# A graph-attention layer with a mixture of experts on one core: the edge stage by destination tile in 34 fixed chunks, with the node update, the router and the dispatch inside its loop

## The reference

```python
x = layernorm(x)                              # inner input; the residual adds the raw x
hh = (x @ W).reshape(n, 8, 32)
s = leaky_relu(s_src[src] + s_dst[dst])       # per head
alpha = softmax of s over the edges of one dst
out = scatter(hh[src] * alpha) + x
x = x_raw + elu(layernorm(out) * gamma + beta)
y = layernorm(x)
logits = y @ gate_w + gate_b                  # 16 experts, top 2, softmax over the two
moe = sum over the 2 chosen e: w_e * (relu(y @ w1[e] + b1[e]) @ w2[e] + b2[e])
x = x + layernorm(y + moe) * gamma2 + beta2
```

## Time and profile before

| what | us |
|---|---|
| median of 3 runs (3936.52 to 3939.79) | 3939.26 |
| span of the profiled execution, first to last instruction | 3974.2 |
| first to last gather of the edge stage begins | 159.9 to 2926.0 |
| stage4 and route together | 2935 to 3300 |
| clearing and lists, experts, last stage | 3300 to 3974 |

### The profile page before, as it was taken

The page is one execution under the profiler, slowest core; times in us unless marked ns, Lnnn a source line. Parts: engine busy times, 40 slices in busy tenths (PEclk is TensorE's granted clock), DMA queues, the critical chain, the costliest instruction groups (busy, mean ns, idle before and its releaser), DMA issues. The chain is left out here.

```text
span 3974.2 us, 63681 instructions
## 1 busy us (share of the span) xinstructions
PE 2665.6 (67%) x11030; PEld 2067.8 (52%) x11031; DVE 1943.5 (49%) x5747; ACT 1154.1 (29%) x4391; POOL 1958.4 (49%) x1920
## 2 busy tenths in 40 slices
PE   5377777777777777776777677777740444999900
PEld 4356556566556655555556555555530442666600
DVE  6355555555545554555545555555569322222246
ACT  4222222222222222222222222222244221333333
POOL 1255565655555665565656556656645451000065
PEclk8676776766777776677777767667765556999955
DMA  4333333333333333333333333333340323333333
GB/s 128 92 82 86 83 85 85 87 84 85 83 83 85 85 87 81 84 84 84 86 84 85 84 83 86 86 81 84 86 129 0 122 74 94 97 96 96 96 99 102
DMA packets 199124, 348.04 MB, mean 88 GB/s; under 512 B 56146, under 2 KB 134976, under 8 KB 199092
## 3 DMA queue, kind: packets, MB, share of 16 engines
q0 software_dynamic: 90432, 259.73, 23.8%
q1 hardware_dynamic: 99636, 87.69, 7.2%
q10 hardware_dynamic: 9024, 0.30, 0.1%
HBM read 301.28 MB, written 46.28 MB: 87 GB/s over the span
## 5 line engine op out<-in xcount | busy, mean ns | idle before, releaser
L849 POOL DMA_INDIRECT gat<-table,idx x1680 | 1663.8, 990 | 1130.7 <-ACT idx L886 638.4
L954 PE MATMUL ps_sum<-msg,hot 128*128 128x264 f32 x3348 | 1363.3, 546 | 0.0
L945 PE MATMUL ps_hot<-ident,hot 128*128 128x128 f32 x1680 | 463.7, 370 | 756.3 <-DVE hot L987 668.6
L954 PEld LDWEIGHTS ps_sum<-msg,hot 128*128 128x128 f32 x3348 | 809.5, 267 | 117.1
L945 PEld LDWEIGHTS ps_hot<-ident,hot 128*128 128x128 f32 x1680 | 266.8, 186 | 1073.3 <-DVE hot L987 676.6
L1002 DVE TENSOR_TENSOR acc<-acc,ps_sum 128x264 f32 x836 | 357.3, 427 | 787.7 <-PE ps_sum L954 446.9
L935 PEld LDWEIGHTS ps_look<-dst_tab,hotT 128*128 128x128 f32 x3356 | 644.7, 268 | 4.7 <-issue 1.3
L935 PE MATMUL ps_look<-dst_tab,hotT 128*128 x3356 | 605.8, 298 | 0.9 <-ACT hotT L905 0.9
L905 ACT ACTIVATE hotT<-ps_hot 128x256 f32<-128x256 f32 x840 | 322.6, 384 | 950.0 <-remote 401.2
L1005 DVE TENSOR_TENSOR msg<-gat,msg 128x512 f32<-128x512 f32 x838 | 577.3, 689 | 17.3 <-ACT msg L900 14.9
L900 ACT ACTIVATE msg<-score 128x16 f32<-128x16 f32 x838 | 180.9, 216 | 1088.7 <-DVE score L993 735.6
(11 more groups left out here) (270 smaller groups left out, 1687.0 us busy)
## 6 DMA issues: line engine op xcount, KB each, us to landing
gat<-table,idx POOLq DMA_INDIRECT x1680
w_sb<-in_L_ffn_w_dram SPq DMA_DIRECT2D x8, 2048.0 KB, 16.5
xt<-dispatched SPq DMA_DIRECT2D x111, 128.0 KB, 2.1
b_t<-in_L_ffn_b_dram SPq DMA_DIRECT2D x109, 128.0 KB, 3.0
expert_out<-o_sb SPq DMA_DIRECT2D x105, 128.0 KB, 1.7
table<-rows SPq DMA_DIRECT2D x49, 128.0 KB, 1.7
x_all<-in_x_dram SPq DMA_DIRECT2D x6, 896.0 KB, 10.3
out_dram<-normed SPq DMA_DIRECT2D x6, 896.0 KB, 4.3
```

What stands on the lines that cost most here:

```text
L849: pool.indirect_dma_start(gat[:, k, j, :], None, table, bass.IndirectOffsetOnAxis(ap=idx[:, k, j:j + 1], axis=0)).then_inc(landed[k], 16)
L945: last = pe.transpose(ps_hot[k % 2][:, j * P:(j + 1) * P], hot[:, k, j, :], ident[:, :])
L954: last = pe.matmul(ps_sum[(k - SUMS) % 2][:, 0:SUM], hot[:, (k - SUMS) % BODY, j, :], msg[:, (k - SUMS) % MSGS, j, :], start=(j == 0), sto ...
```

## The change

The schedule of steps is gone from the edge stage. Its loop now goes over the 49 destination tiles, and each tile takes a window of exactly 34 chunks of 128 edges from the place where its first edge stands in the sorted list (`lo_i`); an edge of another tile in the window gets no one-hot column. Partition p holds 34 edges that follow each other. The window is worked in four groups of 9, 9, 8 and 8 chunks, and one VectorE instruction serves a whole group.

Edges past the window go through `overflow`, which is simple and works one chunk after another, in passes of four. The counts give one such chunk here, so it runs one pass of four chunks. `stage1` finds the first edges with 39 small matmuls and more passes over the edge list, and writes padded copies of the edges to DRAM (`src_pad`, `dst_pad`, and `dst_half` in 16 bits).

The transposes of the one-hot matrices are gone: SyncE loads the window's destinations as one row into all 128 partitions (`dst_row`), and two ScalarE instructions over 4,352 elements turn it into the transposed one-hot matrix `hotT` in bf16. The lookup multiplies that with the destination scores split into three bf16 parts (48 columns), which VectorE adds up. In each of the large VectorE multiplies, compares and adds one operand lies in PSUM (`weight`, `iota`, `looked`). `ps_sum` adds up all 34 chunks of a tile, and the accumulator is added once a tile.

The work of `stage4` and `route` is cut into pieces of one tile (`class Finish`). In tile t of the loop stand pieces for tiles t-1, t-2 and t-3; `last_tiles` does what remains. Both weight loads stand there now, in four quarters each, and TensorE waits in `stage6` for the quarter that its expert needs.

```diff
+NEVER = 20000.0
+WCH = 34
+GROUPS = (9, 9, 8, 8)
+GSTART = (0, 9, 18, 26)
...
-    def step(k, g, head):
-        if not head:
-            pool.wait_ge(msg_ready, g - (BODY - 1))
-        pool.wait_ge(idx_ready, g + 1)
-        pool.sem_inc(pool_turn, 1)
-        for j in range(2):
-            pool.indirect_dma_start(gat[:, k, j, :], None, table,
-                                    bass.IndirectOffsetOnAxis(ap=idx[:, k, j:j + 1], axis=0)).then_inc(landed[k], 16)
...
-        dve.tensor_tensor(hot[:, k, :, :], node_iota[:, :].unsqueeze(1).to_broadcast([P, 2, P]),
-                          rel[:, k, :].unsqueeze(2).to_broadcast([P, 2, P]), ALU.is_equal).then_inc(hot_ready, 1)
...
-        dve.tensor_tensor(msg[:, m, :, 0:D].rearrange("p j (h d) -> p j h d", d=HD),
-                          gat[:, (k - WEIGH) % BODY, :, 0:D].rearrange("p j (h d) -> p j h d", d=HD),
-                          msg[:, m, :, D:SUM].unsqueeze(3).to_broadcast([P, 2, HEADS, HD]),
-                          ALU.mult).then_inc(msg_ready, 1)
...
+# in build(), between stage2 and stage3
+        with nc.cleanup_on_exit():
+            bounds(nc, table, schedule, src_pad, dst_pad, ident, node_iota, neg_first, dst_tab, dst_split,
+                   counts, seg_max)
+            overflow(nc, table, schedule, src_pad, dst_pad, acc, ident, node_iota, neg_first, dst_tab, counts)
+    stage3(nc, table, src_pad, dst_pad, dst_half, dispatched, finish, node_iota, node_id, neg_main, dst_split,
+           lo_i)
...
+# stage3, SyncE
+        lo = sp.value_load(lo_i[0:1, bass.ds(t, 1)], min_val=0, max_val=E)
+        if not head:
+            sp.wait_ge(hotT_ready, t)
+            sp.sem_inc(sp_turn, 1)
+        sp.dma_start(dst_row[:, :], dst_half[bass.ds(lo, WIN)].unsqueeze(0).to_broadcast([P, WIN])).then_inc(row_in, 16)
+        for g in range(NG):
+            if not head:
+                sp.wait_ge(landed[g], t * (16 * GROUPS[g]))
+                sp.sem_inc(sp_turn, 1)
+            sp.dma_start(idx[g][:, :], of_group(src_pad, lo, g)).then_inc(idx_in[g], 16)
+        if not head:
+            sp.wait_ge(rel_ready, t)
+            sp.sem_inc(sp_turn, 1)
+        sp.dma_start(dst_t[:, :], dst_pad[bass.ds(lo, WIN)].rearrange("(p e) -> p e", e=WCH)).then_inc(dst_in, 16)
+# stage3, GpSimd
+    def tile(t, head, old, last=False):
+        for g in range(NG):
+            pool.wait_ge(idx_in[g], t * 16 + 16)
+            pool.sem_inc(pool_turn, 1)
+            if not head:
+                pool.wait_ge(msg_ready, (t - 1) * NG + g + 1)
+                pool.sem_inc(pool_turn, 1)
+            for k in range(GROUPS[g]):
+                pool.indirect_dma_start(gat[:, GSTART[g] + k, :], None, table,
+                                        bass.IndirectOffsetOnAxis(ap=idx[g][:, k:k + 1], axis=0)).then_inc(landed[g], 16)
+            if g == 0 and old >= 3:
+                finish.send(pool, t - 3, dispatched, pool_turn)
+# stage3, ScalarE
+    def rows(t, head):
+        act.wait_ge(row_in, t * 16 + 16)
+        if not head:
+            act.wait_ge(look_done, t * NG)
+        act.activation(hotT[:, :], dst_row[:, :], ACT.Abs, bias=neg_id[:, bass.ds(t, 1)]).then_inc(apart_ready, 1)
+        act.wait_ge(apart_ready, t + 1)
+        act.activation(hotT[:, :], hotT[:, :], ACT.Relu, bias=1.0, scale=-1.0).then_inc(hotT_ready, 1)
+    def tile(t, head, old, last=False):
+        if old >= 1:
+            finish.norm_inner(act, t - 1)
+            finish.root_inner(act, t - 1)
+            if old >= 2:
+                finish.root_outer(act, t - 2)
+            act.preload_act_table(ACT.Exp)
+        for g in range(NG):
+            m, n = g % 2, GROUPS[g]
+            if g == 1 and old >= 1:
+                finish.centre(act, t - 1)
+            if g == 1 and old >= 2:
+                finish.norm_outer(act, t - 2)
+                finish.turned(act, t - 2, ps_t)
+            if g == 2 and old >= 1:
+                finish.lower(act, t - 1)
+            if g == 2 and old >= 2:
+                finish.odds(act, t - 2)
+            if g == NG - 1 and not last:
+                rows(t + 1, False)
+            act.wait_ge(score_ready, t * NG + g + 1)
+            if not (head and g < 2):
+                act.wait_ge(sum_done, t * NG + (g - 1))
+            act.activation(weight[:, m, 0:n, :], score[:, m, 0:n, :], ACT.Exp).then_inc(weight_ready, 1)
+            act.activation(msg[:, m, 0:n, D:SUM], score[:, m, 0:n, :], ACT.Exp).then_inc(denom_ready, 1)
+# stage3, TensorE
+    def look(t, g, head):
+        n, m = GROUPS[g], g % 2
+        if g == 0:
+            pe.wait_ge(hotT_ready, t + 1)
+        if not (head and g < 2):
+            pe.wait_ge(look_read, t * NG + (g - 1))
+        for k in range(n):
+            last = pe.matmul(ps_look[m][:, k * SPLIT * 2 * HEADS:(k + 1) * SPLIT * 2 * HEADS],
+                             by_chunk[:, GSTART[g] + k, :],
+                             dst_split[:, bass.ds(t, 1), :, :].rearrange("p t c h -> p (t c h)"),
+                             start=True, stop=True)
+        last.then_inc(look_done, 1)
+    def total(t, g, head):
+        n, m = GROUPS[g], g % 2
+        pe.wait_ge(hot_ready, t * NG + g + 1)
+        pe.wait_ge(msg_ready, t * NG + g + 1)
+        pe.wait_ge(denom_ready, t * NG + g + 1)
+        if g == 0 and not head:
+            pe.wait_ge(added, t)
+        for k in range(n):
+            last = pe.matmul(ps_sum[:, 0:SUM], hot[:, m, k, :], msg[:, m, k, :],
+                             start=(g == 0 and k == 0), stop=(g == NG - 1 and k == n - 1))
+        last.then_inc(sum_done, 1)
+    def tile(t, head, old, last=False):
+        for g in range(NG):
+            if g < NG - 1:
+                look(t, g + 1, head)
+            elif not last:
+                look(t + 1, 0, False)
+            if g == 1 and old >= 2:
+                finish.vote(pe, t - 2, ps_route)
+            total(t, g, head)
+            if g == 0 and old >= 2:
+                finish.turn(pe, t - 2, ps_t)
+            if g == 1 and old >= 2:
+                finish.ranks(pe, t - 2, ps_route)
+# stage3, VectorE
+    def columns(t, head):
+        dve.wait_ge(dst_in, t * 16 + 16)
+        if not head:
+            dve.wait_ge(hot_ready, t * NG)
+        dve.tensor_scalar(rel[:, :], dst_t[:, :], neg_main[:, bass.ds(t, 1)], None, ALU.add).then_inc(rel_ready, 1)
+    def group(t, g, head):
+        n, m, j = GROUPS[g], g % 2, GSTART[g]
+        early = head and g < 2
+        dve.wait_ge(look_done, t * NG + g + 1)
+        dve.tensor_reduce(looked[:, 0:n, :], ps_look[m][:, 0:n * SPLIT * 2 * HEADS].rearrange(
+            "p (j c h) -> p j h c", c=SPLIT, h=2 * HEADS), AX.X, ALU.add).then_inc(look_read, 1)
+        dve.wait_ge(landed[g], (t + 1) * (16 * n))
+        dve.wait_ge(look_read, t * NG + g + 1)
+        dve.tensor_tensor(both[:, 0:n, :], gat[:, j:j + n, D:ROW], looked[:, 0:n, :], ALU.add).then_inc(both_ready, 1)
+        dve.wait_ge(both_ready, t * NG + g + 1)
+        dve.tensor_reduce(score[:, m, 0:n, :], both[:, 0:n, :].rearrange("p j (c h) -> p j h c", h=HEADS),
+                          AX.X, ALU.max).then_inc(score_ready, 1)
+        if not early:
+            dve.wait_ge(sum_done, t * NG + (g - 1))
+        if g == 0:
+            dve.wait_ge(rel_ready, t + 1)
+        dve.tensor_tensor(hot[:, m, 0:n, :], iota.unsqueeze(1).to_broadcast([P, n, P]),
+                          rel[:, j:j + n].unsqueeze(2).to_broadcast([P, n, P]), ALU.is_equal).then_inc(hot_ready, 1)
+        dve.wait_ge(weight_ready, t * NG + g + 1)
+        dve.tensor_tensor(msg[:, m, 0:n, 0:D].rearrange("p j (h d) -> p j h d", d=HD),
+                          gat[:, j:j + n, 0:D].rearrange("p j (h d) -> p j h d", d=HD),
+                          weight[:, m, 0:n, :].unsqueeze(3).to_broadcast([P, n, HEADS, HD]),
+                          ALU.mult).then_inc(msg_ready, 1)
+    def tile(t, head, old, last=False):
+        columns(t, head)
+        if old >= 1:
+            finish.sums(dve, link, t - 1, ps_sum)
+        for g in range(NG):
+            group(t, g, head)
+            if g == 0 and old >= 1:
+                finish.scale_inner(dve, link, t - 1)
+            if g == 0 and old >= 2:
+                finish.scale_outer(dve, link, t - 2)
+            if g == 1 and old >= 1:
+                finish.lift(dve, link, t - 1)
+            if g == 1 and old >= 2:
+                finish.choose(dve, link, t - 2, ps_route)
+            if g == 2 and old >= 1:
+                finish.join(dve, link, t - 1)
+            if g == 2 and old >= 2:
+                finish.place(dve, link, t - 2, ps_route)
+    link = Chain(dve, dve_chain)
+    dve.tensor_scalar(neg_id[:, :], node_id[:, :], -1.0, None, ALU.mult).then_inc(iota_ready, 1)
+    dve.tensor_copy(iota, node_iota[:, :]).then_inc(iota_ready, 1)
...
+# class Finish
+def sums(self, dve, link, a, ps_sum):
+    num = self.num[:, 0:D]
+    heads = num.rearrange("p (h d) -> p h d", d=HD)
```

(61 more changed lines are left out.)

1307 lines of the change are left out of this document (631 added, 676 removed).

## The result

The changed kernel took 4180.7 us (4179.7 to 4181.5, 4 runs) beside 3937.9 us before (3935.7 to 3939.8): ratio 1.062, 95% interval 1.061 to 1.064. It is slower, where 3,200 us, so faster, was forecast. Later runs of the same pair of kernels on another chip gave the opposite sign, 0.934; the experiments tell how that came out. First comes the profile of the slow execution: of the page the first rows and those of GpSimd and of the clock, then the groups that matter (busy us, mean ns, then the idle time before them and its releaser). They stand beside the earlier trace rows of before.

A forecast was written before the change was run, and what follows sets the result against it. GpSimd's gathers were taken as the highest floor, with ring, clock and relay adding the rest. 3974 - 2775 - 365 + 77 + 2260 + 16 + 36 + 6 = 3229 us of span, so 3,200 us; range 3,130 to 3,500.

The forecast's parts named there:

- The loop over tiles is priced by its fullest engine: Edge loop: GpSimd's 34 gathers and 2 sends set 46.2 us a tile, the other engines' work fitting beside them.
- The sum itself: Whole kernel: 3974 - 2775 - 365 + 77 + 2260 + 16 + 36 + 6 = 3229 us of span.
- the front: Work ahead of the loop: stage1 18, bounds 4 and overflow 55 us added, first loop gather near 237 us.
- the loop: 49 tiles at 46.2 us, less three pairs of sends that fall behind the loop: 2,260 us.
- what lies behind it: After the loop: 16 us behind the last gather, 36 for last_tiles and 6 for experts and weights added; 732 in all.
- The others: Per tile of the loop: VectorE 30 us, TensorE 26 to 42, ScalarE's two large instructions at most 13, DMA some 40%.
- The port: Edge loop: large VectorE instructions with one SBUF input do not block GpSimd, which keeps its 46.2 us a tile.
- The ring rival: Edge loop: waits among TensorE, VectorE and ScalarE set the pace, not GpSimd; 51.5 us a tile, 3,460 us; chance 0.25.
- The slower rival: Edge loop: large VectorE instructions hold up gathers; 62.3 us a tile, 3,990 us; chance 0.08.
- relay: Old edge stage: ScalarE and VectorE wait until SyncE issues its list load and passes arrivals on; about 0.5 us a step.

The follow-up runs named there:

- e2: Changed kernel with ScalarE's copy of the turned row after group 1's exponentials and TensorE's router products after group 1's sums: 4086.4 us, 64.5 us a tile on chip A.
- four pauses: Changed kernel with GpSimd waiting after each group's gathers until all have landed: 3680.4 us, 55.9 us a tile on chip A; 3670.4 us on C.

## Why the prediction was wrong, point by point

- **The step that failed** is in "The loop over tiles is priced by its fullest engine": that the work of VectorE, TensorE and ScalarE lies beside the gathers at its own durations. On chip A it doesn't. The durations held, but the overlap failed: TensorE's signals come up to 27 us late while GpSimd gathers without a pause, `yT` and all behind it wait, and the send then waits 21 us for its slots. So a tile takes 66.4 us, where 46.2 was forecast and chip C gives 45.2. From first to last gather that is 3,214 us on A against 2,207 on C: 1,007 of the 1,029 us between the two spans (4178.0 and 3148.7). The kernel before loses to the same kind of chip, but less: 3,937 us on A against 3,354 on C, 583 us. So the changed kernel loses more than it saves on A; where signals are prompt nothing is lost, and the sign is the one that was forecast (0.934 on D). What makes the signals late, and why on these chips, is not known.
- **The sum itself** holds where signals are prompt: 3,229 us of span against 3148.7 on chip C. Of the 80 us too many, 22 are the front (237 against a first gather at 215.3), 53 the loop (2,260 against 2,207 from first to last gather), 6 what lies behind it (732 against 726). On A the front was 214.6, the loop 3,214 and the rest 749 us.
- **GpSimd**: 46.2 us a tile forecast, 45.2 on C, of which 34.3 busy.
- **The others**, per tile, from ten tiles of chip C:

```profile
680.00:1132.10 452.10, 262.07 (x1120) 209.76 (x1118) 276.29 (x616) 149.87 (x200) 342.52 (x360) 0.76 0.47 136
```

 The columns are TensorE, weight loads, VectorE, ScalarE, GpSimd, the granted clock, the DMA share and GB/s. VectorE has 27.6 us (30 forecast), TensorE 26.2 (26 to 42), ScalarE 15.0 (up to 21; its two large ones take 3.9 and 3.8 us, 7.7 instead of at most 13), DMA 47% (some 40).
- **The port.** A gather beside the 2.54 us multiply with one operand in PSUM keeps its 0.95 us, here on chip A. The Trainium skill's page "SBUF — State Buffer", section "Who interferes with whom", says that a VectorE instruction with at most one SBUF input, outside two-port modes, does not contend with GpSimd; the trace agrees.

```profile
1552.66 2.54 DVE L1224 TENSOR_TENSOR msg<-gat,ps_weight 128x2304 f32<-128x2304 f32 x1
1552.69 0.95 POOL L1100 DMA_INDIRECT gat<-table,idx  x1 [0.30 <-issue]
1553.94 0.95 POOL L1100 DMA_INDIRECT gat<-table,idx  x1 [0.30 <-issue]
```

- **The rivals.** The ring rival named ScalarE's copy of the turned row ahead of the exponentials, the very place of the wait; but it priced 51.5 us a tile, and the order, the part of its reasons that e2 tested, was worth 2.0 us a tile. The slower rival had the sign, and a time 190 us short (3,990), with the wrong mechanism: no gather was held up (951 ns in the mean). Its sign is luck.
- **The sign that was missed** stood in the trace of before. ScalarE and VectorE stood still 4 us at a time until SyncE's issue was through the earlier trace rows; I called this a relay, and that reading was wrong. ScalarE's copy waited for the signal of TensorE's transposes, which stands at 1508.14, 0.02 us ahead of the copy. Four signals of TensorE due at 1502.8 to 1505.6 are freed within 0.2 us there (1508.09 to 1508.26), the first 5.3 us late, and an instruction of SyncE of 0.7 us lies in the same stretch. The relay's 0.5 us a step, which the change was to save, was this lateness at least in part. With the denser gathers of the changed kernel it grew.

## What to carry to other kernels

Time a change on more than one chip: the same pair of kernels stands at 1.062 on one and at 0.934 on another, both with intervals far from one. Before pricing a loop by its fullest engine, look whether signals arrive when instructions end. Three marks went together here: "remote" as a releaser, register instructions of 0.7 us on an engine that has nothing to do, and signals of several TensorE instructions within 0.2 us. They say that the waits of the profile are not those that the program's order makes. Where they appear, letting GpSimd's gathers run out every 8 to 11 is worth a trial: it took 12% off the changed kernel in one run on A, and it costs 2.7 us each time ((55.9 - 45.2) / 4), so 17% where signals are prompt.

## What the runs showed of the hardware that was not expected

On two of five chips (A, E) TensorE's signals come late while GpSimd issues indirect gathers every 1.25 us; in the traces taken on the three others (B, C, D) none is over 0.02 us late. On A SyncE's records are themselves late: the packets of one `dst_t` load ran from 1574.96 to 1575.69 us, and the record of its issue begins at 1576.11. And on A records are missing: of the landings the trace of the changed kernel holds 12,659 events, on C 41,754; with four pauses on A 24,971. The signals of VectorE and ScalarE lack records too (226 of 810 and 215 of 618 in the changed kernel's loop on A, none on C). So the path on which signals and records travel may be what fills up, but that is only argued: no run tested it, and why TensorE's signals alone are late it doesn't say. The Trainium skill, "NOTIFIC — the notification-queue block", section "Overflow: three behaviours, one of which stalls the engine", says that inside the block that writes such records producers are held back rather than a record lost, which could stall an engine, while a full ring in memory discards new records in one of its modes. Held-back signals and missing records would fit the two, but no run here shows that either took place. Every timed run here carries a recorded clock, so whether a run that records nothing would be slow on A was not tried. It stays open, as does what distinguishes the chips.
